# Attention of a two-layer kernel: maxima of unit 0 ahead of sequence 1's projections, and sixty filler products

## What is computed

```python
x = x * 0.1
nx = _ln(x, g_ln1, b_ln1)
q = _heads(nx @ W_sq + b_sq, B)       # 16 heads of 8 features
k = _heads(nx @ W_sk + b_sk, B)
v = _heads(nx @ W_sv + b_sv, B)
s = jnp.einsum('bhqd,bhkd->bhqk', q, k) * SCALE
p = jax.nn.softmax(s, axis=-1)
so = _merge(jnp.einsum('bhqk,bhkd->bhqd', p, v), B) @ W_so + b_so
x = x + so
```

## Time and profile before

| | |
|---|---|
| median of 3 runs | 463.72 us (462.73 to 465.2) |
| profiled execution | 462.69 us |
| its span | 460.9 us |
| mean granted TensorE clock | 0.885 of full |
| PE busy | 354.5 us, 77% of the span |
| DVE busy | 264.5 us, 57% |
| ACT busy | 201.7 us, 44% |
| POOL busy | 114.1 us, 25% |
| chain that ended last | PE 58%, DVE 15%, issue 8%, ACT 6%, DMA 6%, POOL 5% |

### The profile page before, as it was taken

How to read it: one execution, slowest core, us unless ns; L and a number is a source line. 1 busy time by engine, 2 the same in 40 slices (tenths; PEclk the granted TensorE clock), 3 DMA queues, 4 the chain that set the end, 5 groups by cost and what they waited for, 6 DMA issues and landing times.

```text
span 460.9 us, 6703 instructions
## 1 busy us (share of the span) xinstructions
PE 354.5 (77%) x2495; PEld 209.4 (45%) x2495; DVE 264.5 (57%) x661; ACT 201.7 (44%) x317; POOL 114.1 (25%) x155
## 2 busy tenths in 40 slices
PE   1797302995189899899999799987873899989970
PEld 0576301995133322233221467554463443677850
DVE  5425500332687598788950758544568947883435
ACT  2332100321040477677778458564624335565210
POOL 2000277156050716311110000010000055462232
PEclk9997555998579999999999779999995799899987
DMA  4599114001326656000000000001999467431232
GB/s 113 152 192 320 46 52 117 13 33 40 105 63 181 143 144 160 1 3 2 2 2 2 0 0 1 1 1 36 371 329 290 148 201 248 152 106 37 60 82 46
DMA packets 35876, 46.01 MB, mean 100 GB/s; under 512 B 4778, under 2 KB 21682, under 8 KB 35844
## 3 DMA queue, kind: packets, MB, share of 16 engines
q1 hardware_dynamic: 33156, 38.57, 29.9%
q0 software_dynamic: 2688, 7.02, 5.3%
HBM read 31.67 MB, written 13.78 MB: 99 GB/s over the span
## 4 chain that ended last, share of the span: by engine, by line
PE 58%; DVE 15%; issue 8%; ACT 6%; DMA 6%; POOL 5%; SPq 1%; POOLq 0%; DVEq 0%; ACTq 0%
PE ps L1397 9%; PE ps L1605 6%; PE ps L1591 5%; PE ps L1566 4%; PE ps L1851 4%; PE ps L1515 3%; PE ps L1574 3%; PE ps L1696 3%; PE ps L1880 3%; DVE early L1210 3%; PE ps L1527 2%; POOL disp_d L538 2%; PE ps L1801 2%; DVE xn L982 2%; PE ps L1786 2%
## 5 line engine op out<-in xcount | busy, mean ns | idle before, releaser
L1210 DVE TENSOR_REDUCE early<-ps 128x1 f32<-128x512 f32 x128 | 81.0, 684 | 15.9 <-PE ps L1566 11.7
L755 ACT ACTIVATE R<-ps 128x1024 f32<-128x1024 f32 x64 | 62.7, 1020 | 24.7 <-PE ps L1591 23.7
L1397 PE MATMUL ps<-ident,R 128*77 128x128 f32 (+1 forms) x224 | 35.3, 296 | 31.8 <-DMA R<-disp_d 24.8
L1397 PEld LDWEIGHTS ps<-ident,R 128*77 128x77 f32 (+1 forms) x224 | 26.7, 152 | 50.4 <-DMA R<-disp_d 25.2
L1566 PE MATMUL ps<-R 72*128 72x512 bf16 x112 | 39.0, 382 | 1.1 <-DVE early L1210 0.2
L1591 PE MATMUL ps<-R 75*128 75x512 bf16 x128 | 37.6, 379 | 1.6 <-DMA R<-R 1.3
L621 POOL DMA_INDIRECT R<-h_d,srow x16 | 16.5, 1033 | 77.3 <-DMA h_d<-ff 70.3
L1605 PE MATMUL ps<-R,vaug 128*9 128x512 f32 x256 | 33.5, 595 | 0.6 <-ACT R L755 0.6
L1179 DVE TENSOR_SCALAR R<-ps,vcol 128x256 f32<-128x256 f32 x16 | 7.0, 479 | 37.7 <-PE ps L1515 37.7
L1566 PEld LDWEIGHTS ps<-R 72*128 72x128 bf16 x112 | 10.8, 96 | 33.1 <-DVE early L1210 23.9
L538 POOL DMA_INDIRECT disp_d<-R,srow x16 | 15.9, 993 | 36.7 <-DVE srow L1125 32.1
(11 more groups left out here) (324 smaller groups left out, 696.2 us busy)
## 6 DMA issues: line engine op xcount, KB each, us to landing
R<-in_L_ffn_W_dram SPq DMA_DIRECT2D x1, 6144.0 KB, 19.9
h_d<-R SPq DMA_DIRECT2D x12, 256.0 KB, 2.8
q_d<-R SPq DMA_DIRECT2D x24, 96.0 KB, 1.9
R<-k_d SPq DMA_DIRECT2D x24, 96.0 KB
R<-q_d SPq DMA_DIRECT2D x8, 288.0 KB
R<-in_L_ffn_w_dram SPq DMA_DIRECT2D x1, 2048.0 KB, 17.1
h_d<-ff SPq DMA_DIRECT2D x6, 256.0 KB, 2.5
disp_d<-R SPq DMA_DIRECT2D x1, 1032.0 KB, 12.8
```

Of the source, the lines that this page charges most:

```text
L755: s.activation(probs[idx % 4], ps[:, 2 * (idx % 2):2 * (idx % 2) + 2, :].rearrange("p b t -> p (b t)"), ACT.Exp, scale=QK_SCALE).then_inc( ...
L1210: v.tensor_reduce(mcol[:, u, col:col + 1], bank(ring_bank("row", n)), AX.X, ALU.max).then_inc(s1_max, 1)
L1397: return m.transpose(dst, src, ident[0:k, 0:k])
```

## The change

On PE sixty products of 512 columns (`spin(512)`) into bank 1, with nothing to wait for, stand ahead of sequence 0's transposes. Row tiles 16 and 17 come before `max_transpose(0)`; sequence 1's transposes follow it at once, and its key, query and value products come one by one behind tiles 19, 21 and 23. The fillers of 256 columns stay behind tiles 24 to 27 alone. `ring_order` is changed to match. On DVE `scale_of` is cut in two: for sequence 1 only the factors are made ahead of the maxima, its four tiles are scaled behind maxima 2, 5, 8 and 11, and sequence 0's value bias moves behind maximum 16. On SP `load_max(1)` moves ahead of the last six query stores of sequence 1.

```diff
--- before.py
+++ after.py
@@ -333,7 +333,7 @@
 
 
 
-        ring_order = [("row", n) for n in range(MU)] + [("max", 0)] + [("row", n) for n in range(MU, LEAD)]
+        ring_order = [("row", n) for n in range(MU + 2)] + [("max", 0)] + [("row", n) for n in range(MU + 2, LEAD)]
         for st in range(TB * UNITS + 1):
             ring_order += [("row", n) for n in range(LEAD + 4 * st, LEAD + 4 * st + 3) if n < MU * UNITS]
             if st % TB == 1 and st // TB + 1 < UNITS:
@@ -456,9 +456,11 @@
             for hg in range(HG):
                 store_keys(1, hg)
             sp.wait_ge(q_parts, 2)
-            for hg in range(HG):
-                store_queries(1, hg)
+            store_queries(1, 0)
+            store_queries(1, 1)
             load_max(1)
+            store_queries(1, 2)
+            store_queries(1, 3)
             for hg in range(HG):
                 load_packed(1, hg)
             for u in range(2, UNITS):
@@ -970,7 +972,7 @@
                                             ALU.mult, ALU.add))
                 v.tensor_scalar(var_eps[:, 0, half], mv[:, half, 1], LN_EPS, None, ALU.add).then_inc(ln_stats, 1)
 
-            def scale_of(src, dst, i, b, again=False):
+            def scale_factors(i, b, again=False):
 
                 half = slice(b * TB, (b + 1) * TB)
                 dve.wait_ge(ln_std, 2 * i + b + 1)
@@ -978,9 +980,15 @@
                 me.link(v.reciprocal(rstds[:, 0:k, half], std[:, 0:k, half]))
                 if again:
                     me.link(v.tensor_scalar(rstds[:, :, half], rstds[:, :, half], 0.1, None, ALU.mult))
+
+            def scale_tile(src, dst, t, again=False):
+                v.tensor_scalar(dst[:, t, 0:D], src[:, t, :], mv[:, t, 0:1], rstds[:, int(again), t:t + 1],
+                                ALU.subtract, ALU.mult).then_inc(ln_out, 1)
+
+            def scale_of(src, dst, i, b, again=False):
+                scale_factors(i, b, again)
                 for t in range(b * TB, (b + 1) * TB):
-                    v.tensor_scalar(dst[:, t, 0:D], src[:, t, :], mv[:, t, 0:1], rstds[:, k - 1, t:t + 1],
-                                    ALU.subtract, ALU.mult).then_inc(ln_out, 1)
+                    scale_tile(src, dst, t, again)
 
             def layer_norm(src, dst, i, again=False):
                 for b in range(B):
@@ -1193,7 +1201,10 @@
                 if t % TB == TB - 1:
                     dve.wait_ge(x2_ready, t + 1)
                     stats(x2, 2, t // TB, again=True)
-                    scale_of(x2, xn, 2, t // TB, again=True)
+                    scale_factors(2, t // TB, again=True)
+                    if t < TB:
+                        for tile in range(TB):
+                            scale_tile(x2, xn, tile, again=True)
 
             def add_value_bias(b):
 
@@ -1220,9 +1231,13 @@
                                 rden[:, :].rearrange("p (t h) -> p t h", h=4).unsqueeze(3).to_broadcast([P, TB, 4, HD]),
                                 ALU.mult).then_inc(o_norm, 1)
 
-            add_value_bias(0)
+
             for n in range(LEAD):
                 row_max(n)
+                if n < MU and n % 3 == 2 and n // 3 < TB:
+                    scale_tile(x2, xn, TB + n // 3, again=True)
+                if n == MU:
+                    add_value_bias(0)
             n = LEAD
             for st in range(TB * UNITS + 1):
                 for i in range(4):
@@ -1536,13 +1551,12 @@
                                    wx[:, W_SV, :], start=True, stop=True)
                 ins.then_inc(v_mm, 1)
 
-            def project_keys_queries(b):
-                transpose_tiles(xn, ln_out, 2 * T, ln_tp, [b])
+            def project_heads(b, n):
+
                 pe.wait_ge(xT_ready, 4 + b + 1)
-                for n, (w, bk) in enumerate(((1, 3), (0, 2))):
-                    if b:
-                        pe.wait_ge(qk_ready, masked[3] if n else K_0)
-                    m.matmul(bank(bk), wx_qk[:, w, :], xT[:, b * SEQ:(b + 1) * SEQ], start=True, stop=True).then_inc(qk_mm, 1)
+                if b:
+                    pe.wait_ge(qk_ready, masked[3] if n else K_0)
+                m.matmul(bank(3 - n), wx_qk[:, 1 - n, :], xT[:, b * SEQ:(b + 1) * SEQ], start=True, stop=True).then_inc(qk_mm, 1)
 
             def ring_free(kind, k):
 
@@ -1619,16 +1633,29 @@
 
                 m.matmul(ps[:, 1, 0:columns], ones_b[:, :], zeros[:, 0:columns // 2].bitcast(BF16), start=True, stop=True)
 
-            project_keys_queries(0)
+            for i in range(60):
+                spin(512)
+            transpose_tiles(xn, ln_out, 2 * T, ln_tp, [0])
+            project_heads(0, 0)
+            project_heads(0, 1)
             project_values(0)
             for r in range(MU):
                 first_row_tile(r)
+            score_row_tile(MU)
+            score_row_tile(MU + 1)
             max_transpose(0)
-            project_keys_queries(1)
-            project_values(1)
-            for n in range(MU, LEAD):
+
+            transpose_tiles(xn, ln_out, 2 * T, ln_tp, [1])
+            for n in range(MU + 2, LEAD):
                 score_row_tile(n)
-                spin(256)
+                if n == MU + 3:
+                    project_heads(1, 0)
+                elif n == MU + 5:
+                    project_heads(1, 1)
+                elif n == MU + 7:
+                    project_values(1)
+                elif n > MU + 7:
+                    spin(256)
             def row_tiles(n, count):
 
                 for k in range(n, min(n + count, MU * UNITS)):
```

## The result

The changed kernel takes 469.8 us in the median of four runs (467.0 to 473.5), the kernel before 464.1 beside it. The ratio is 1.013, with a 95% interval of 1.007 to 1.018: slower, by 3.3 to 8.5 us. The profiled execution of the changed kernel is its fastest run, 467.0 us with a span of 465.2, 4.3 us above that of before; the 2.8 us from there to the median lie in runs that have no profile.

A forecast was written before the change was run, and what follows sets the result against it. Bound by a chain of VectorE's lead-tile maxima, a never-idle TensorE, then the `load_max(2)` DMA landing at 185.49. 0.6 later at stage 8 plus 1.9 of clock: 2.5 us slower, 466.2 against the median, range 460.5 to 469.3.

The forecast's parts named there:

- step 6: Start of attention stage 0 (S): waits for `load_max(0)`, 156.5, 4.0 us earlier; half clock adds 1.25 to unit 1's transpose.
- the term of the sum for the landing of `load_max(2)`: Load that stage 8 (unit 2) waits for: lands at 186.1, 0.6 us later than before.
- Step 1: Sixty products ahead of sequence 0's transposes: 13.0 us, hidden by TensorE's wait; full clock brings keys 1.2 us earlier.
- Step 2: ScalarE and GpSimd after the keys: 0.3 us gained for row tile 0, 0.9 for query split and sequence 0's packed loads.
- Steps 3 to 5: Row stage: first maximum at 131.9, last at 145.45 (4.4 us gained); sequence 1's queries by 156.4, tiles to 27 by 152.6.
- Step 7: SP: `load_max(1)` holds six query stores until 163.75, so sequence 1's packed loads start at 169.8, against 169.19.
- Step 8: Stage 8: `load_max(2)` lands at 186.1; TensorE arrives at 180.9 and waits over 5 us, where it waited 1.27.
- Step 9: Clock after the wait at stage 8: half clock costs 1.9 us, bounds 0 and 2.7.
- Rival A: Clock holds in both waits, nothing lost after stage 8: 0.6 us faster, 463.1; chance 0.18.
- Rival B: Small loads of the maxima pass the packed ones: 461.8 for `load_max(0)` alone, 454.2 with `load_max(2)` too; chance 0.21.
- C: Sixty products run at half clock, 25.6 us, making everything from the transposes on 12 us late: 475.7; chance 0.04.
- rival D: Further waits, such as a late tile 16 or half clock twice, double the loss: about 469; chance 0.09.

The follow-up runs named there:

- e7: The kernel before with the sixty unread products alone added: 461.2 us against 461.0, ratio 1.003.
- e8: The changed kernel without the sixty products: ratio 1.014 to the kernel before.
- e11: e5 without the sixty products ahead of the transposes: 457.3 us (kernel before 466.2), ratio 0.984.
- e1: The changed kernel with sequence 1's transfers in the old order, all twelve query stores before `load_max(1)`: 464.6 us against 465.3 before, ratio 0.995.
- e4: The kernel before with only `load_max(1)` moved between the query stores of sequence 1: 472.5 us, ratio 1.018.
- e3: The changed kernel with the old order of sequence 1's transfers and 24 fillers behind row tile 27: 461.1 us, ratio 0.990 to the kernel before.
- e2: The changed kernel with 24 more unread products of 512 columns behind row tile 27: 471.1 us, ratio 1.014 to the kernel before.
- e5: e3 with 14 fillers, unit 0's maxima loaded ahead of sequence 0's packed group 3, unit 2's ahead of sequence 1's groups 2 and 3: 456.4 us against 461.0, ratio 0.994.
- e6: e5 with the maxima of unit 2 behind all packed loads of sequence 1, as in the kernel before: 460.2 us, too few runs for a ratio.
- e9: e5 without its 14 fillers behind row tile 27: 458.3 us (kernel before 466.2), ratio 0.985.
- e12: e5 again, unchanged, on the same chip as e9, e10 and e11: 458.7 us (kernel before 466.2), ratio 0.984.
- e10: The kernel before with only the transfers in the order of e5: 463.0 us against 466.2, ratio 0.996.

## Why the prediction was right and wrong

The direction held, narrowly: chances of 0.40 for slower and 0.42 for no difference stood behind it. 2.5 us slower was forecast, 3.3 to 8.5 measured, and the median of 469.8 lies just above the range. Of the mechanism, what happens on SyncE held: stores behind its wait, and a gain that is swallowed at stage 8. The clock was put in the wrong place. The step that failed is step 6, the start of stage 0 and the clock behind it; through it the term of the sum for the landing of `load_max(2)`, 0.6, became 4.4. The other term, 1.9 for the clock behind stage 8, was charged and did not occur. The two errors partly cancel, which is luck: without the second the sum would have been 0.6. Step by step:

- Step 1 held in its cost (110 to 123, hidden) and not in its use. The transposes gained 0.15 us, but the clock fell again behind them (0.57 from 126 to 130) and the keys still waited 2.09 us, against 2.16 in the earlier trace rows. e7, e8 and e11 find no effect on the time.
- Step 2 failed: the query split gained 0.35 us and not 0.9, and the packed loads of sequence 0 behind the last query stores went out at 146.62, 1.1 us later than before (145.50) and not 0.9 earlier.
- Steps 3 to 5 held. The first maximum came at 132.2 (131.9 foreseen), the maximum transpose of unit 0 at 146.04 (145.5), tile 27 at 152.6 (152.6), the query parts of sequence 1 at 156.46 (156.4).
- Step 6 failed in both its terms. S was foreseen at 156.5 and came at 159.2; 2.0 of these 2.7 us are the packed loads of step 2, where the last query store took 4.06 us to land. Why it did stays open: of all fourteen profiles this one has these packed loads latest behind the first transpose, 22.54 us against 21.0 to 22.4. e1 and e8, with the same order up to there, had S at 157.4 and 158.4. The larger failure is the clock: half clock "for part of stages 0 and 1", 1.25 us, was foreseen; it lasted to 174, and TensorE reached stage 8 at 188.7, where 180.9 was foreseen. The maxima of unit 1 were ready at 168.0 instead of 163.75, 2.7 of it from S and 1.5 from the clock.
- Step 7 held: 6.05 us from the parts of unit 1 to the first packed load were foreseen, 6.3 measured. e4 and e1 show it by itself, in both directions: 6.25 us with the stores between, 1.87 without.
- Step 8: the landing of `load_max(2)` came 15.6 us behind the first packed load (16.3 foreseen), hence at 189.9 instead of 186.1. This is the term of the sum that was too small, 4.4 instead of 0.6, and it inherits its error from step 6. The wait of 5 us was not there (1.23), because half clock had delayed TensorE just as much.
- Step 9 was charged at the wrong place. There was no half clock behind stage 8; it came behind stage 0. Where the main loop starts at full clock and TensorE then waits at stage 8, as in e3, e2 and e4, it does come there: the part of D from stage 8 on is 1.6, 2.9 and 5.1 us longer, where I took 1.9 and at most 2.7. The Trainium skill's rule that products resume at half rate after a wait for a transfer ("TensorE: Matmul & The Clock Gate", "HAM oscillation — how this bites in real kernels") holds in its direction there; the estimate of 0.8 us for a restart drawn from its case is far below what these three runs show. The waits of 1.27, 1.23 and 1.03 us at stage 8 (before, the changed kernel, e8) were followed by full clock.
- Rival A fell (the clock did not hold). Rival B fell too: the small loads of the maxima did not pass the packed ones, and took 6.33 and 5.41 us to land. e5 and e6 take them past by order of issue, but stage 0 doesn't wait there because fillers cover the time: e9, with the order of e5 and no fillers, waits 3.98 us. C did not happen (the sixty products took 13.11 us at full clock); rival D, further loss from the clock, is the nearest to what was measured.

## What to carry to other kernels

Before a wait is moved forward on a queue that issues transfers, list what stands behind it: here six stores whose data were ready waited 8.8 us for a small load that nobody needed before stage 4. A gain ahead of a transfer-bound point is only worth what that point moves, and a tensor engine that arrives early may lose more to its clock than it won. So put the transfers right first, then reorder the engines. Unread products in what is left of a wait, up to the dense work, kept the clock at 1.00 in e2, e5 and e12; what they are worth in time is not shown here, and sixty of them 8 us ahead of the dense tiles brought nothing.

## What was not expected of the hardware

- Half clock outlasted the wait by a length that varied much, with TensorE busy all the time: after waits of 6.10, 4.22, 4.27 and 4.88 us it stood at 0.50 for another 15, 14, 6 and 11 us (the changed kernel, e1, e2, e4). After 2.31 us it was 3.4 (e3), but after only 1.59 us some 9 (e7), so the length of the wait doesn't set it alone. I had expected some 4.
- Small loads of 4 KB issued up to 2.5 us behind packed ones took 4.2 to 7.8 us to land, against the 1.7 us that they take alone. Some 3 us behind them it was anything from 1.8 (e10, unit 0) to 5.4 (before, unit 2), and 6.7 us behind them 1.8 (e1, unit 2).
